# Mixture-of-experts block: the first layer's weighted rows stored in tile order and gathered per token

## The chip, the cores and the metric

The kernel runs on one core of one Trainium2 chip. The metric is the device time of one execution in microseconds; lower is better. The kernel before was timed three times: 865.56, 866.69 and 867.43 us, median 866.69 us.

## The reference

The input is `x`, 8 sequences of 512 tokens with 128 features. Three sublayers follow each other, each on a layer norm of `x`: half a feed-forward layer, causal attention with 16 heads, and the same half feed-forward layer again.

```
x = x + 0.5 * ffn(layernorm(x))
x = x + attention(layernorm(x))
x = x + 0.5 * ffn(layernorm(x))        # the same weights

ffn(x):  xn       = layernorm(x) * gamma + beta
         abel_out = gelu(xn @ abel_w + abel_b)
         topw, topi = top_k(xn @ moe_gate_w + moe_gate_b, 2); topw = softmax(topw)      # 8 experts
         expert e(t) = gelu(xn @ ew1[e] + eb1[e]) @ ew2[e] + eb2[e]                     # 128 -> 256 -> 128
         moe_out  = (sum over the token's two experts of topw * expert) @ expm(g0) @ expm(g1) @ expm(g2)
         gate     = sigmoid([abel_out, moe_out] @ gc_w + gc_b)
         return x + abel_out * (1 - gate) + moe_out * gate
```

## The kernel before, in words

**Units.** A chunk `c` is one sequence of 512 tokens (four tiles of 128). Both feed-forward layers route: each token is written twice, once per chosen expert, into the DRAM tensor `z_rows`, in the region of its expert. A row has 132 numbers: 128 features, the expert's weight, the row's own place (`Z_PLACE`, which says to which token and pick it belongs), and two spare ones. So an expert's rows lie together, and tiles of 128 rows with one expert each are read back. There are 80 tiles in a layer; four tiles are a quad (20 quads), two are a pair (`p`, 40 pairs). Rows of chunks 0 and 1 make run 0 in the first layer (quads 0 to 5), those of chunks 2 to 7 run 1 (quads 6 to 19).

**The expert stage** goes over the pairs. For each quad SyncE (SP) reads the tiles' starts from a table and issues four transfers of 66 KB into one of six x buffers (`load_x`, L654). TensorE transposes the quad (`x_turn`, L2080) at pair 2(q-1), ScalarE writes it (L1112), TensorE multiplies by `w1` of the tile's expert (`up`, L2106), ScalarE applies gelu (L1133), TensorE multiplies by the second matrix, which already holds the rotation (`down`, L2120 and L2122), and VectorE weights the rows into one of five y buffers (`y_out_`, L1630), two pairs behind in its own list. VectorE also copies the `w1` of each tile to a ring of five (L1677), three to four tiles ahead of its pair number. In its program order TensorE's pair `p` is `up(p)`, then the transposes if `p` is even, then `down(p-1)`, then what stands beside it.

**What becomes of y.** GpSimd (POOL) sends each tile of y with an indirect transfer to `y_rows`, which is ordered by token and pick; the index is the `Z_PLACE` column in the x buffer (`send_y`, L833). The x buffer of quad q-6 is free, and `load_x(q)` goes out, when these four have landed (`y_sent`). When a run is complete SP reads a chunk's pairs back with one plain transfer of 528 KB (`load_sums`, L618), after `load_x(0, 11)` for chunks 0 and 1, after the operands of batch 0 for chunk 2, and within the attention batches for the rest. `sum_pairs` adds the two picks of each token, and `finish_x` applies the gate and adds to `x`: on VectorE for chunks 0 and 1 (at p = 21 to 24 of its list), on GpSimd for chunks 2 to 7.

**Attention** goes over 8 batches of 40 units. The scores are computed twice, first for the row maxima (VectorE, L1757 to L1762), a batch ahead, then for the exponentials (ScalarE, L1194). For batch 0 SP writes the first half of the operands (`operands`, L541, L547, L551: 15 small transfers and one for zeros) as soon as VectorE has split q and k (`q_k_low(0)`, at p = 34), and TensorE starts the maxima's scores of batch 0 (L2204) when they have landed and its experts are done. In a batch GpSimd cuts the causal triangle out of the exponentials (`triangle`, L864; three instructions a call, eight calls a batch), and TensorE's products with v (`values`, L2276) wait for it. Between the triangles GpSimd sends the second layer's rows (`send_z`, L783): the first pick behind the last triangle of a batch, the second between the first two of the next.

**Other transfers.** During the first experts ScalarE's queue brings the attention's position biases, 1 MB each, at pairs 4, 6, 10, 12, 14, 16, 18, 20, 36 and 38 (`load_bias`, L1060, L1070). They and SP's transfers use queues q10 and q1 of the same 16 DMA engines; GpSimd's use q0.

The lists of all engines are written out by hand; `beside_experts` has, per engine, what stands at which pair.

## Time and profile before

| | us |
|---|---|
| median of three runs | 866.69 |
| the profiled execution's own time | 872.2 |
| its span | 870.4 |
| TensorE busy in the span | 684.1 (79%) |
| VectorE / ScalarE / GpSimd busy | 563.2 / 414.2 / 495.2 |
| indirect transfers of y, both layers (L833), GpSimd | 160 in 163.9 |

All durations below are from the one profiled execution. Its own time is 1.8 us above its span and 5.5 us above the median of the runs, so a sum is made against 872.2 us, and the same difference is then taken off the median. TensorE's granted clock over the span is 0.918 of full speed. The stages of the span: preparation to 118 us, the first experts from 135 to 264 us, the maxima of batch 0 from 268 to 295 us, the eight attention batches to about 690 us, then the second experts.

### The profile page before, as it was taken

The page shows a single profiled execution, that of the slowest core. Times are in us where ns is not written, and L with a number is a line of the kernel's source. Part 1 is how long each engine was busy: PE and PEld are TensorE (multiplying, and loading weights), DVE is VectorE, ACT ScalarE, POOL GpSimd, SP SyncE. Part 2 cuts the span into 40 slices and gives each one's busy share as a digit, 9 for nine tenths or more (in the row PEclk, how much of TensorE's full clock was granted, in tenths as well). Part 3 has the DMA queues.
Part 4 walks back from the last instruction along what each step waited for, and adds up shares of the span by engine and source line. Part 5 has one row for each costly group of instructions (what it writes and reads, how often), then busy time and mean ns, then how long its engine had stood idle before and what let it go on. Part 6 is the DMA issues. An engine that isn't in the chain of part 4 may idle for free.

```text
span 870.4 us, 18357 instructions
## 1 busy us (share of the span) xinstructions
PE 684.1 (79%) x5103; PEld 511.4 (59%) x5103; DVE 563.2 (65%) x2051; ACT 414.2 (48%) x931; POOL 495.2 (57%) x600
## 2 busy tenths in 40 slices
PE   1568637985898798999999999999986828888850
PEld 0468626875795564665656566565653418778850
DVE  3678852865857875776768677676772204687574
ACT  2246204543471264565655656555654715636530
POOL 2557773773685162456837477463545544567772
PEclk9969967997998998999999999999997969979985
DMA  8613342895257403114041230302100145333365
GB/s 243 198 42 91 101 108 75 230 254 183 71 135 188 128 21 93 24 27 128 2 120 35 51 103 16 95 9 69 49 14 29 34 115 140 98 89 93 105 213 165
DMA packets 84143, 86.59 MB, mean 99 GB/s; under 512 B 14561, under 2 KB 66412, under 8 KB 83692
## 3 DMA queue, kind: packets, MB, share of 16 engines
q1 hardware_dynamic: 64952, 50.14, 22.3%
q0 software_dynamic: 9312, 21.58, 7.3%
q10 hardware_dynamic: 9780, 13.69, 6.2%
q8 instruction: 45, 0.74, 0.4%
q14 instruction: 54, 0.44, 0.2%
HBM read 46.23 MB, written 31.92 MB: 90 GB/s over the span
## 4 chain that ended last, share of the span: by engine, by line
PE 48%; DVE 20%; issue 9%; DMA 7%; SPq 7%; ACT 4%; POOL 2%; ACTq 2%; DVEq 1%; POOLq 0%
PE bank L2276 8%; PE bank L2204 8%; PE bank L2251 7%; PE bank L2106 5%; DMA arena<-z_rows 3%; PE bank L2120 3%; PE pair L2047 3%; DVE mx L1757 2%; POOL y_rows L833 2%; SPq L551 2%; DVE mx L1759 2%; DMA y_rows<-arena 1%; PE bank L2080 1%; SPq L654 1%; DVE stat L1277 1%
## 5 line engine op out<-in xcount | busy, mean ns | idle before, releaser
L1194 ACT ACTIVATE arena<-bank 128x512 f32<-128x512 f32 x320 | 185.9, 600 | 168.9 <-PE bank L2251 166.1
L833 POOL DMA_INDIRECT y_rows<-arena x160 | 163.9, 1025 | 106.0 <-DVE arena L1630 70.7
L864 POOL TENSOR_SCALAR_AFFINE_SELECT arena<-arena 128x256 f32<-128x256 f32 (+1 forms) x192 | 94.6, 516 | 173.9 <-ACT arena L1194 173.8
L2204 PE MATMUL bank<-kZ,qT 128*128 128x512 f32 (+3 forms) x512 | 148.3, 357 | 14.1 <-DVE mx L1760 5.5
L2251 PE MATMUL bank<-qT,kZ 128*128 128x512 f32 (+3 forms) x512 | 155.9, 376 | 2.7 <-DMA qT<-mT_zero 2.0
L1133 ACT ACTIVATE arena<-bank,hidden_bias 128x128 f32<-128x128 f32 x320 | 91.3, 368 | 93.0 <-PE bank L2106 88.7
L2204 PEld LDWEIGHTS bank<-kZ,qT 128*128 128x128 f32 x512 | 87.5, 196 | 61.5 <-issue 17.9
L1757 DVE TENSOR_REDUCE mx<-bank 128x1 f32<-128x512 f32 x128 | 87.2, 681 | 41.4 <-PE bank L2178 40.4
L2106 PE MATMUL bank<-arena 128*128 128x128 f32 x640 | 95.1, 295 | 15.1 <-DVE arena L1677 8.9
L2120 PE MATMUL bank<-w_rot,arena 128*128 x640 | 100.9, 296 | 5.2 <-ACT arena L1133 5.2
L2276 PE MATMUL bank<-arena,vA 128*9 128x512 f32 (+3 forms) x1024 | 95.5, 453 | 11.8 <-issue 6.4
L2251 PEld LDWEIGHTS bank<-qT,kZ 128*128 128x128 f32 x512 | 84.8, 197 | 25.6 <-ACT arena L1194 11.1
L2106 PEld LDWEIGHTS bank<-arena 128*128 128x128 f32 x640 | 83.7, 204 | 22.7 <-issue 21.1
L783 POOL DMA_INDIRECT z_rows<-beside_kZ,place x80 | 78.7, 983 | 31.3 <-issue 22.0
L2120 PEld LDWEIGHTS bank<-w_rot,arena 128*128 128x128 f32 x640 | 89.7, 201 | 8.1 <-issue 6.4
L1677 DVE COPY arena<-w 128x256 f32 x160 | 46.6, 316 | 64.8 <-issue 35.8
L1759 DVE TENSOR_REDUCE mx<-bank 128x1 f32<-128x384 f32 x128 | 70.0, 547 | 16.4 <-PE bank L2181 16.1
L1630 DVE TENSOR_SCALAR arena<-bank,arena 128x132 f32<-128x132 f32 x160 | 48.8, 345 | 25.4 <-PE bank L2122 25.3
L2080 PE MATMUL bank<-ident,arena 128*128 128x128 f32 x160 | 28.2, 307 | 47.0 <-DMA arena<-z_rows 30.4
L1112 ACT ACTIVATE arena<-bank,cols 128x512 f32<-128x512 f32 x40 | 31.7, 792 | 64.4 <-PE bank L2080 64.4
L1762 DVE TENSOR_REDUCE mx<-bank 128x2 f32<-128x512 f32 x64 | 43.6, 681 | 18.2 <-PE bank L2184 13.3
L783 POOL DMA_INDIRECT z_rows<-w,place x48 | 46.8, 975 | 13.2 <-issue 11.3
(269 smaller groups left out, 1172.1 us busy)
## 6 DMA issues: line engine op xcount, KB each, us to landing
arena<-z_rows SPq DMA_DIRECT2D x160, 66.0 KB
kZ<-bias_k_r ACTq DMA_DIRECT2D x8, 1024.0 KB, 10.3
qT<-parts SPq DMA_DIRECT2D x42, 128.0 KB
kZ<-parts SPq DMA_DIRECT2D x168, 32.0 KB
sums<-y_rows SPq DMA_DIRECT2D x7, 528.0 KB, 5.2
beside_kZ<-y_rows SPq DMA_DIRECT2D x7, 528.0 KB, 7.6
y_rows<-arena POOLq DMA_INDIRECT x160
z_rows<-in_spare SPq DMA_DIRECT2D x4, 528.0 KB, 6.1
```

The lines of the kernel that those rows point to most:

```text
L783: g_.indirect_dma_start(z_rows[run], bass.IndirectOffsetOnAxis(place[g % DEEP][:, k, t:t + 1], 0), zz(g)[:, k, t, :], None).then_inc(z_sen ...
L833: g_.indirect_dma_start(y_rows[run], bass.IndirectOffsetOnAxis(x_[:, t, Z_PLACE:Z_PLACE + 1].bitcast(I32), 0), y_[:, t, :], None).then_inc ...
L864: g_.affine_select(out=cut, in_=cut, compare_op=ALU.is_ge, fill=0.0, base=0, pattern=[[0, 2], [0, blocks], [1, P]], channel_multiplier=-1) ...
L1133: a_(hid[p % 2][:, i, j, :], ps_up[p % 2][:, P * n:P * (n + 1)], ACT.Gelu, bias=hidden_bias[:, j, bass.ds(e, 1)]).then_inc(hidden_ok.sem, 1)
L1194: a_(dst, src, ACT.Exp).then_inc(exp_ok.sem, 1)
L1757: v.tensor_reduce(mx[:, 3, q, t:t + 1], src[:, :], AX.X, ALU.max).then_inc(reduced.sem, 1)
L1759: v.tensor_reduce(mx[:, 2, q, t:t + 1], src[:, 0:384], AX.X, ALU.max)
L2106: last = mm(into, tile(w1_e, j), tile(xnT[q % 2], t), start=True, stop=True)
L2120: mm(into, hid[p % 2][:, i, j, :], w2_rot[:, bass.ds(e, 1), j, :].rearrange("p a n -> p (a n)"), start=(j == 0), stop=False)
L2204: mm(outp, qT[u][:, t, query_tile * P:(query_tile + 1) * P], kZ[u][:, h, 0:keys], start=start, stop=False, skip_group_check=(kind != "full"))
L2251: return mm(outp, kZ[u][:, h, lo:lo + P], qT[u][:, t, lo:SEQ], start=start, stop=True, skip_group_check=(kind != "full"))
L2276: last = mm(ps_o[32 * q:32 * q + HD + 1, kb * P:SEQ], vA[u][:, kb, NG * q + t, :], pT[t % 2][:, q, PT_KB[kb]:PT_KB[kb] + n], start=(kb == ...
```

## The change

It concerns the first layer only; the second still scatters its y as before.

- `y_rows` of runs 0 and 1 are now in the order of the tiles. SP stores a whole quad with one plain transfer of 264 KB (`store_y`), once its four tiles are weighted, and signals `y_kept`. In SP's list `store_y(q-6)` stands ahead of `load_x(0, q)`, which no longer waits for anything sent. Quads 14 to 17 are stored ahead of the operands of batch 0, quads 18 and 19 behind them.
- The 80 indirect sends of the first layer go from GpSimd. In their place it gathers, per chunk, two picks of four tiles, each with an indirect transfer of 128 rows (66 KB), straight into the terms of the sum (`gather`): 64 for the eight chunks. Chunks 0 and 1 are gathered when quads 1 to 5 are stored, chunk 2 when quad 19 is and chunk 0 is finished, chunk 3 when chunk 2 is finished, chunks 4 to 7 in batches 0 to 3, two transfers behind each of the four last triangle calls.
- Where a row lies in tile order is worked out by VectorE: the place in the expert's region minus the expert's offset (`y_places`, three instructions per run, at p = 2 and p = 4). For this the picks and the places of the eight chunks are kept.
- `load_sums` of the first layer is gone; only the 256 KB of gelu terms of chunks 2 to 7 are still loaded (`load_abel_act`). Chunk 2 uses the buffers of chunks 3 to 7 rather than its own.
- On VectorE `sum_pairs(0, 0)` moves from p = 21 to 20, `sum_pairs(0, 1)` from 22 to 23, `finish_x(0, 0)` from 23 to 22, `finish_x(0, 1)` from 24 to 25, and the preparation of attention on all engines is two pairs earlier.
- ScalarE's first exponential waits for the last five stores where it waited for chunk 2.

```diff
--- before.py
+++ after.py
+    z_rows = dram_rows("z_rows", [(REGION + P) * E] * len(RUN_CHUNKS))
+    y_rows = dram_rows("y_rows", [NT * P * SWITCH[0], NT * P * (QUADS - SWITCH[0])] + [SPARE + 2 * E * P] * 2)
...
             n = QUADS * layer + q
-            engine.wait_ge(y_sent[n % Y_BUFS], 16 * NT * (n // Y_BUFS + 1))
+            if n < QUADS:
+                engine.wait_ge(y_kept[n % Y_BUFS], 16 * (n // Y_BUFS + 1))
+            else:
+                engine.wait_ge(y_sent[n % Y_BUFS], 16 * NT * len(range(n, QUADS - 1, -Y_BUFS)))
...
+            def load_abel_act(c):
+
+                if c == 2:
+                    wait(sp, y_weighted, 0)
+                else:
+                    x_done(sp, 0, c - 1)
+                sp.wait_ge(ab_stored, 16 * CH)
+                sp.dma_start(terms(0, c)[1], abel_act[SEQ * c:SEQ * (c + 1), :].rearrange("(t p) d -> p t d", p=P)
+                             ).then_inc(abel_act_in, 16)
+
...
+            def store_y(q):
+
+                run, n = run_of_quad(0, q)
+                up_to(sp, y_weighted, 0, NT * (q + 1))
+                sp.dma_start(y_rows[run][NT * P * n:NT * P * (n + 1), :].rearrange("(t p) n -> p t n", p=P),
+                             y_buffer(0, q)).then_inc(y_kept[q % Y_BUFS], 16)
...
-                if q >= X_BUFS:
+                if layer and q >= X_BUFS:
                     y_sent_up_to(sp, layer, q - X_BUFS)
...
             for q in range(X_BUFS, QUADS):
+                store_y(q - X_BUFS)
                 load_x(0, q)
-                if q == SWITCH[0] + X_BUFS - 1:
-                    load_sums(0, 0)
-                    load_sums(0, 1)
+            for q in range(QUADS - X_BUFS, QUADS - 2):
+                store_y(q)
             operands(sp, 0, 0, 0)
-            load_sums(0, 2)
+            for q in range(QUADS - 2, QUADS):
+                store_y(q)
+            load_abel_act(2)
...
-                    load_sums(0, b + 3)
+                    load_abel_act(b + 3)
...
+            def gather(c, picks=(0, 1), tiles=range(NT)):
+
+                run = run_of_chunk(0, c)
+                if 0 in picks and 0 in tiles:
+                    wait(pool, y_placed, run)
+                    last = SWITCH[0] if run == 0 else QUADS
+                    for q in range(last - Y_BUFS, last):
+                        y_sent_up_to(pool, 0, q)
+                    if c == 0:
+                        wait(pool, tabled, 1)
+                    if c >= 2:
+                        x_done(pool, 0, 0 if c == 2 else c - 1)
+                for k in picks:
+                    for t in tiles:
+                        g_.indirect_dma_start(terms(0, c)[0][:, t, k, :], None, y_rows[run],
+                                              bass.IndirectOffsetOnAxis(y_place[:, c, k, t:t + 1], 0)
+                                              ).then_inc(sums_in[1 if c == 1 else 0], 16)
...
-                if layer == 0:
-                    if p == 25:
-                        attention_roots(0)
-                        attention_roots(1)
-                    if p == 31:
-                        obias(0)
-                    if p == 34:
-                        obias(1)
-                    if p == 36:
-                        v_place(0, 0)
...
+            def first_experts():
+
+                for b in range(2):
+                    gather(b)
+                for b in range(2):
+                    attention_roots(b)
+                obias(0)
+                obias(1)
+                v_place(0, 0)
+                gather(2)
+                sum_pairs(0, 2)
+                finish_x(0, 2)
+                gather(3)
...
-                triangle(b, 2, 0)
-                triangle(b, 2, 2)
-                triangle(b, 3, 0)
-                triangle(b, 3, 2)
+                for i in range(4):
+                    triangle(b, 2 + i // 2, 2 * (i % 2))
+                    if b + 4 < BATCH:
+                        gather(b + 4, (i // 2,), range(2 * (i % 2), 2 * (i % 2) + 2))
...
-                    x_done(act, 0, 2)
-                    wait(act, y_weighted, 0)
+                    for quad in range(QUADS - Y_BUFS, QUADS):
+                        y_sent_up_to(act, 0, quad)
...
+            def y_places(r):
+
+                run, c = Run(dve, y_placed, r), slice(SPLIT[0] * r, SPLIT[0] if r == 0 else CH)
+                wait(dve, tabled, r)
+                n = RUN_CHUNKS[r] * 2 * NT
+                picks = pick_of[:, c, :, :, :].rearrange("p c k t e -> p (c k t) e")
+                run.step(v.tensor_tensor(picks, picks, offsets[r][:, 0:E].unsqueeze(1).to_broadcast([P, n, E]), ALU.mult))
+                run.join()
+                run.step(v.tensor_reduce(y_shift[:, c, :, :].rearrange("p c k t -> p (c k t)"), picks, AX.X, ALU.add))
+                run.join()
+                run.step(v.scalar_tensor_tensor(y_place[:, c, :, :], y_shift[:, c, :, :], -1.0, place_of[:, c, :, :], ALU.mult, ALU.add))
...
-                    if p == 21:
+                    if p == 2:
+                        y_places(0)
+                    if p == 4:
+                        y_places(1)
+                    if p == 20:
                         sum_pairs(0, 0)
                     if p == 22:
-                        sum_pairs(0, 1)
-                    if p == 23:
                         finish_x(0, 0)
                         attention_stats(0)
-                    if p == 24:
+                    if p == 23:
+                        sum_pairs(0, 1)
+                    if p == 25:
                         finish_x(0, 1)
                         attention_stats(1)
+                    if p == 26:
+                        attention_norm(0)
                     if p == 28:
-                        attention_norm(0)
+                        x_low(0)
                     if p == 30:
-                        x_low(0)
+                        attention_norm(1)
                     if p == 32:
-                        attention_norm(1)
+                        q_k_low(0)
                     if p == 34:
-                        q_k_low(0)
-                    if p == 36:
                         x_low(1)
...
-                    for b, at in ((0, 29), (1, 35)):
+                    for b, at in ((0, 27), (1, 33)):
```

SP's list around the first operands, before; `qT` and `kZ` are the operands, `oT` holds the split q and k, and the last x quad is ahead of the first row:

```order
L654 DMA arena<-z_rows 128x132
L541 DMA qT<-mT_zero 8x2x512
L547 DMA qT<-oT 32x2x512
L551 DMA kZ<-oT 8x2x512 x4
L547 DMA qT<-oT 32x2x512
L551 DMA kZ<-oT 8x2x512 x4
L547 DMA qT<-oT 32x2x512
L551 DMA kZ<-oT 8x2x512 x4
L618 DMA arena<-y_rows 128x4x264
L621 DMA arena<-abel_act 128x4x128
```

The same place on SP after; `y_rows<-arena` is a stored quad:

```order
L671 DMA arena<-z_rows 128x132
L639 DMA y_rows<-arena 128x4x132 x4
L553 DMA qT<-mT_zero 8x2x512
L559 DMA qT<-oT 32x2x512
L563 DMA kZ<-oT 8x2x512 x4
L559 DMA qT<-oT 32x2x512
L563 DMA kZ<-oT 8x2x512 x4
L559 DMA qT<-oT 32x2x512
L563 DMA kZ<-oT 8x2x512 x4
L639 DMA y_rows<-arena 128x4x132 x2
L622 DMA w<-abel_act 128x4x128
```

Four stores, of quads 14 to 17, now stand between the last x transfer and the first operand.

GpSimd's list from the last triangles of batch 1 to the second triangle of batch 2, before:

```order
L864 AFFINE_SELECT arena<-arena 128x2x128 x2
L864 AFFINE_SELECT arena<-arena 128x2x256
L864 AFFINE_SELECT arena<-arena 128x2x128
L783 DMA z_rows<-w,place 34816x132 x4
L864 AFFINE_SELECT arena<-arena 128x2x128
L864 AFFINE_SELECT arena<-arena 128x2x256
L864 AFFINE_SELECT arena<-arena 128x2x128
L783 DMA z_rows<-w,place 34816x132 x4
L864 AFFINE_SELECT arena<-arena 128x2x128
```

The same place after; `sums<-y_rows,y_place` is a gather:

```order
L905 AFFINE_SELECT arena<-arena 128x2x128
L905 AFFINE_SELECT arena<-arena 128x2x256
L905 AFFINE_SELECT arena<-arena 128x2x128
L819 DMA sums<-y_rows,y_place 128x132 x2
L802 DMA z_rows<-w,place 34816x132 x4
L905 AFFINE_SELECT arena<-arena 128x2x128
L905 AFFINE_SELECT arena<-arena 128x2x256
L905 AFFINE_SELECT arena<-arena 128x2x128
L802 DMA z_rows<-w,place 34816x132 x4
L905 AFFINE_SELECT arena<-arena 128x2x128
```

Two gathers now stand between the last triangle of the batch and the four sends of z.

## Rows read from the trace of the kernel before

**Rows 1.** Busy time by stretch; columns: PE, PEld, DVE, ACT, POOL, clock, DMA share, GB/s.
```profile
164.00:208.00 44.00, 29.42 (x238) 27.53 (x238) 28.78 (x113) 18.86 (x58) 28.17 (x27) 0.89 0.92 252
398.00:450.00 52.00, 49.38 (x375) 31.25 (x376) 38.72 (x121) 30.33 (x57) 33.33 (x46) 1.00 0.25 65
```

**Rows 2.** Waits, 134 to 270 us: total us, times, longest.
```profile
PE bank L2080 <- DMA arena<-z_rows: 14.1, 5, 9.5
```

**Rows 3.** Timeline of TensorE: start, us, line, [idle before it, releaser].
```profile
162.53 1.13 PE L2106 MATMUL bank<-arena 128*128 128x128 f32 x8 [0.23 <-ACT arena L1133]
172.35 1.13 PE L2106 MATMUL bank<-arena 128*128 128x128 f32 x8 [0.30 <-ACT arena L1133]
...
197.18 1.13 PE L2106 MATMUL bank<-arena 128*128 128x128 f32 x8
207.81 1.11 PE L2080 MATMUL bank<-ident,arena 128*128 128x128 f32 x4 [9.51 <-DMA arena<-z_rows]
...
215.96 1.13 PE L2106 MATMUL bank<-arena 128*128 128x128 f32 x8
...
222.40 2.05 PE L2106 MATMUL bank<-arena 128*128 128x128 f32 x8 [2.85 <-DVE arena L1677]
```

**Rows 4.** SP's own waits from 118 to 280 us, then its timeline.
```profile
SPq L650 <- DMA y_rows<-arena: 32.4, 9, 8.2
```
```profile
168.18 3.65 SPq L654 DMA_DIRECT2D arena<-z_rows  x4
179.25 9.57 SPq L654 DMA_DIRECT2D arena<-z_rows  x8
```

**Rows 5.** DMA queues, 164 to 208 us: packets, MB, share of the engines.
```profile
q10 hardware_dynamic: 3168, 6.29, 54.9%
q1 hardware_dynamic: 4966, 2.92, 26.2%
q0 software_dynamic: 850, 1.79, 10.9%
```

**Rows 6.** Chain that ended last: start, us, what was waited for.
```profile
171.16 10.38 DMA arena<-z_rows
...
186.72 2.21 DMA y_rows<-arena
```

**Rows 7.** Timeline of VectorE.
```profile
170.07 0.62 DVE L1630 TENSOR_SCALAR arena<-bank,arena 128x132 f32<-128x132 f32 x2
...
201.43 0.71 DVE L1605 TENSOR_TENSOR sums<-sums 128x528 f32<-128x528 f32 x1 [4.40 <-DMA sums<-y_rows]
...
254.21 0.62 DVE L1630 TENSOR_SCALAR arena<-bank,arena 128x132 f32<-128x132 f32 x2 [0.69 <-PE bank L2122]
```

**Rows 8.** Groups by line on GpSimd, 134 to 265 us, then its timeline.
```profile
L833 POOL DMA_INDIRECT y_rows<-arena x73 | 75.9, 1040 | 55.1 <-DVE arena L1630 40.5 <-issue 14.5
```
```profile
169.10 1.16 POOL L833 DMA_INDIRECT y_rows<-arena  x1 [0.30 <-issue]
```

**Rows 9.** Timelines of SP and of TensorE where attention starts.
```profile
250.12 0.93 SPq L541 DMA_DIRECT2D qT<-mT_zero  x1
...
258.92 3.14 SPq L551 DMA_DIRECT2D kZ<-oT  x4
```
```profile
264.40 0.22 PE L2122 MATMUL bank<-expert_bias,fixed 128*128 x1
268.16 0.80 PE L2204 MATMUL bank<-kZ,qT 128*128 128x512 f32 x1 [3.54 <-DMA kZ<-oT]
```

**Rows 10.** Timelines of GpSimd and TensorE at the start of batch 2.
```profile
400.02 1.09 POOL L783 DMA_INDIRECT z_rows<-w,place  x1 [0.19 <-issue]
...
405.87 1.40 POOL L864 TENSOR_SCALAR_AFFINE_SELECT arena<-arena 128x256 f32<-128x256 f32 x3 [0.96 <-ACT arena L1194]
...
412.22 1.40 POOL L864 TENSOR_SCALAR_AFFINE_SELECT arena<-arena 128x256 f32<-128x256 f32 x3
```
```profile
412.89 1.05 PE L2276 MATMUL bank<-arena,vA 128*9 128x512 f32 x8
```

More of the change, by code:

```diff
@@ L166, in macaron_block, with dram_rows @@
                   ident_c, bias_q_c, bias_k_c, fixed_c, spare_c, out):
-    z_rows, y_rows = ([nc.dram_tensor(f"{n}{run}", (rows_, ROW), FP32, kind="Internal").ap() for run in range(len(RUN_CHUNKS))]
-                      for n, rows_ in (("z_rows", (REGION + P) * E), ("y_rows", SPARE + 2 * E * P)))
+    def dram_rows(name, counts):
+        return [nc.dram_tensor(f"{name}{run}", (n, ROW), FP32, kind="Internal").ap() for run, n in enumerate(counts)]
+    z_rows = dram_rows("z_rows", [(REGION + P) * E] * len(RUN_CHUNKS))
+    y_rows = dram_rows("y_rows", [NT * P * SWITCH[0], NT * P * (QUADS - SWITCH[0])] + [SPARE + 2 * E * P] * 2)
     abel_in, abel_act = (nc.dram_tensor(n, (CH * SEQ, D), FP32, kind="Internal").ap() for n in ("abel_in", "abel_act"))
@@ L235, in macaron_block @@
         n_of = tiles_of = sb("n_of", [P, E])
-        first_tile, offset, jump = (sb(n, [P, E + 1]) for n in ("first_tile", "offset", "jump"))
+        first_tile, jump = (sb(n, [P, E + 1]) for n in ("first_tile", "jump"))
+        offsets = [sb(f"offset{i}", [P, E + 1]) for i in range(2)]
         tables = [sb(f"table{i}", [P, 2, MOST_TILES], I32) for i in range(2)]
@@ L441, in macaron_block @@
         abel_added = Steps(sem("abel_added"), 10 * CH)
-        sums_in = [sem(f"sums_in{i}") for i in range(3)]
+        y_placed = Steps(sem("y_placed"), 3)
+        abel_act_in = sem("abel_act_in")
+        y_kept = [sem(f"y_kept{i}") for i in range(Y_BUFS)]
+        sums_in = [sem(f"sums_in{i}") for i in range(2)]
         last_sums_in = [sem(f"last_sums_in{c}") for c in range(CH)]
@@ L526, in sums_in_up_to @@
             if layer == 0:
-                i, n = ((c, 32 if c == 2 else 16) if c < 3 else (0, 16 + 32 * (c - 2)))
+                one = 16 * 2 * NT
+                i, n = (c, one) if c < 2 else (0, one * c)
+                if c >= 2:
+                    engine.wait_ge(abel_act_in, 16 * (c - 1))
                 engine.wait_ge(sums_in[i], n)
@@ new lines, in load_abel_act, with load_sums @@
+            def load_abel_act(c):
[6 more added lines that the diff above has]
+                             ).then_inc(abel_act_in, 16)
+            def load_sums(c):
+                if c in (0, SPLIT[1]):
+                    last = SWITCH[1] if c == 0 else QUADS
+                    for q in range(last - Y_BUFS, last):
+                        y_sent_up_to(sp, 1, q)
+                pairs = y_rows[run_of_chunk(1, c)][2 * SEQ * c:2 * SEQ * (c + 1), :].rearrange(
+                    "(t p k) n -> p t (k n)", t=NT, p=P)
+                sp.dma_start(terms(1, c)[0].rearrange("p t k n -> p t (k n)"), pairs).then_inc(last_sums_in[c], 16)
@@ L825, in experts, with beside_experts @@
-            def experts(layer):
+            def beside_experts(p):
+                if p == 4:
+                    gate_roots(2 * CH - 1, 1)
+                    gate_roots(2 * CH - 1, 0)
+                if 14 <= p < 18:
+                    send_z(2 * CH - 1, ((p - 14) // 2,), range(2 * (p % 2), 2 * (p % 2) + 2))
+            def first_experts():
[10 more added lines that the diff above has]
+                gather(3)
@@ L915, in _ @@
             skip_roots_(1)
-            experts(0)
-            sum_pairs(0, 2)
-            finish_x(0, 2)
+            first_experts()
             over_batches(pool, batch)
-            experts(1)
+            experts()
         @block.scalar
@@ L1547, in gate_place @@
                     z_sent_up_to(dve, g - DEEP)
-                run.step(v.tensor_copy(place[g % DEEP][:, :, :], place_f[:, :, :]))
+                run.step(v.tensor_copy(place[g % DEEP][:, :, :], into))
                 run.end()
@@ L1566, in make_table @@
                 run = Run(dve, tabled, r)
-                layer, n, table = r // 2, 2 * NT * RUN_CHUNKS[r] + E, tables[r % 2]
+                layer, n, table, offset = r // 2, 2 * NT * RUN_CHUNKS[r] + E, tables[r % 2], offsets[r % 2]
                 wait(dve, counted, r)
@@ L2357, in beside_experts @@
                 if layer == 0:
-                    for b, at in ((0, 29), (1, 35)):
+                    for b, at in ((0, 27), (1, 33)):
                         if p == at:
```

64 lines of the change are left out of this document (22 added, 42 removed).

## The prediction, written before the changed kernel was timed

> **What bounds the kernel now.** I read the busy time by stretch first, then the waits of the stretch that stands out, then the timelines of the engines that meet there. In the attention batches TensorE is busy 49.38 of 52.00 us and the DMA engines a quarter of the time [rows 1]: there a wait of TensorE's is paid in full, and transfers are cheap. From 164 to 208 us, in the middle of the first experts, it is the reverse: TensorE is busy 29.42 of 44.00 us and the DMA engines 0.92 of the time [rows 1]. TensorE waits there for x quads, 14.1 us in five waits, the longest 9.5 us [rows 2].
>
> How much is lost there can be read from the starts of `up`. From pair 10 (162.53) to pair 14 (172.35) a pair takes 9.82/4 = 2.45 us. Pair 22 starts at 197.18, pair 25 at 215.96, pair 26 at 222.40 [rows 3]. At 2.45 us from pair 14 they would stand at 191.9, 199.3 and 201.7. So 16.7 us are lost by pair 25 and 20.7 us by pair 26; no change to this stage is worth more than 20.7 us.
>
> Two things make the loss. First, a quad of x is asked for late: SP waits 32.4 us in nine waits for scattered y [rows 4]. The send at 169.10 is the last of quad 4 [rows 8], and SP's next x transfer, which needed it, goes out at 179.25 [rows 4]. Second, what is asked for arrives slowly, since q10 with the biases has 54.9% of the engines, q1 26.2% and q0 10.9% [rows 5]: a quad whose last transfer had been issued at 171.16 lands 10.38 us later [rows 6], and quad 12, queued behind the two loads of sums, is waited for 9.51 us at 207.81 [rows 3].
>
> **The middle of the first experts.** Removed from POOL here are the sends, 73 in this stage at 1.040 us [rows 8] plus 0.30 us of issue each, 1.34 us. None of it is on TensorE's path by itself; what is on it is x waiting for them. Now x of quad q goes out right behind the weighting of quad q-6. Quad 5 is weighted at 170.7 (170.07 + 0.62) [rows 7], so x of quad 11 is asked for at about 173 and not behind 185. The two loads of sums, 1.06 MB, are no longer in front of quad 12.
>
> What comes late next is the gather. `sum_pairs(0, 0)` stands at VectorE's p = 20, which it reaches about when TensorE has done pair 19, 172.35 + 6 x 2.45 = 187 us; VectorE then stands until chunk 0 is there, and behind it in its list are the copies of w1 for pairs 22 and on, so TensorE stops at pair 22. The time is: quad 5 lands (L), eight gathers, the last one's landing, and 1.7 us for the sum (0.71 us for its first instruction [rows 7], about as much for the second long one, and a copy of w1). Then eight more gathers for chunk 1 and the same again for pair 25. No row shows a gather; the nearest is the scatter, 1.34 us each [rows 8], so eight take 10.7 us. A scatter's landing has 2.21 us [rows 6] as its lower end; the upper is 7.5 us, since 179.25 less about 1.5 us of SP's table reads is 7.5 us behind the end of the send at 169.10 + 1.16 [rows 4, 8]. I take 4 us for the first, 3 us for the second.
>
> L is the unknown that decides. The store of quad 5 can be issued at 171.3. If it were served at once it would land 2 to 3 us later, but ahead of it in q1 stand parts of x quad 9, y of quad 4 and x quad 10, and from 165 on the biases take their share. q1 carried 4966 packets in 44 us [rows 5], 113 a microsecond; a quad stored and a quad loaded are 512 rows each. About 1800 such packets from 166 us on are 16 us, so L = 182, and 2 us more for the slowest engine give 184. The bounds are 178 (q1 gets the share that q0 had too) and 190 (it gets a third less).
>
> With L = 184: chunk 0 issued at 195, landed at 199, pair 22 at about 201; chunk 1 issued at 205.7, landed at 208.7, pair 25 at 208.7 + 1.7 = 210.4, against 215.96. That is 5.5 us earlier. Pair 26 lost another 4 us before (6.44 us against 2.45), 2.85 of it waiting for VectorE [rows 3], which then had two finishes and two statistics in two pairs. They now stand at p = 22 and 25, and I count 2 us as won. In sum -7.5 us. With L = 178 it is 6 us more, -13.5; with 190 pair 25 comes at 216.4, and -1.5 is left.
>
> **Added on VectorE:** six small instructions of `y_places`, on 128 and 384 numbers, beside pairs 2 and 4, where its list has no other work. The nearest row is 0.71 us for 528 numbers [rows 7], so they are below 6 x 0.71 = 4.3 us, and I take 2 us in two places. VectorE is busy 28.78 of 44.00 us even in the fuller stretch that follows [rows 1], and is up to two pairs ahead with w1. I take 0; without that cover it would be 2 us.
>
> **The start of attention.** SP starts the operands of batch 0 at 250.12 and issues the last four from 258.92 to 262.06, 11.9 us in all; TensorE's experts end at 264.6 and it starts at 268.16, 3.54 us after waiting for them [rows 9]. Now `store_y(17)` stands ahead, which needs pair 35 weighted. Before, that is at 254.21 + 0.62 = 254.8 [rows 7], which is 9.8 us before the experts' end. Since the projections of batch 1 are now two pairs earlier, 1.5 us of them no longer lie between, so it is 8.3 us before the end. Then 0.6 us for the store and 11.9 us of operands: the last is issued 4.2 us after the experts' end, where it was 2.5 us before it. That is 6.7 us later. Before, the last landed 6.1 us behind its issue (268.16 - 262.06), with two biases of 1 MB under way; those keep their pairs and are through by then, so that the least landing of a transfer, 2.2 us as in [rows 6], is nearer. The start is then 6.4 us behind the experts' end and not 3.5: +3 us (bounds 2 and 6.7). Nothing hides it: VectorE and TensorE both have only the maxima to do, and the first exponentials wait for them.
>
> The gather of chunk 2 (issued once quad 19 has landed), its sum and finish, and the gather of chunk 3 are two times 10.7 us and some 10 us between, from about 7 us behind the experts' end. GpSimd is done by 38 us behind it. The first triangle comes behind the maxima (27 us, from 6.4 us behind the end on), their transfer and five exponentials, at about 40. I take 0; the cover is the maxima of batch 0, and without it all 10.7 us of chunk 3 would count.
>
> **The batches.** POOL gets eight gathers in each of batches 0 to 3, 10.7 us beside 18.7 us of idle time (52.00 - 33.33) [rows 1]. That hides them where the idle time lies behind them. At the end of the batch it does not: there two gathers, 2.6 us, stand ahead of four sends of z and the first triangle of the next batch. At batch 2 the sends began at 400.02, the triangle at 405.87 after 0.96 us of idle time, the second triangle at 412.22 with none, and TensorE's `values` at 412.89, right behind its first third (412.22 + 0.47) [rows 10]. So 2.6 - 1.0 = 1.6 us of delay reach that triangle, and 1.4 to 1.6 us TensorE. This holds for batches 2, 3 and 4 (batch 1 has no sends in front): 3 x 1.4 = +4.2 us. The bounds are 0 (a gather is issued faster than a scatter) and 6.
>
> **The sum:** -7.5 + 3 + 4.2 = -0.3 us on the profiled execution's 872.2, so 871.9; on the median of 866.69, 866.4. I say 866.
>
> A rule speaks on L. In rows, x alone in q1 was slow while q10 was full [rows 5, 6]. The Trainium skill, "DMA: Bandwidth & Descriptors", section "Queues, rings and completion order", says that each DMA engine takes turns between the queue rows that have work and serves a ring in order. By that rule y in q1 gives up q0's turn and stands ahead of x. It would move L and quad 11 towards the late bound, where the bytes alone (264 KB either way) would leave them alone. The trace agrees so far that x waited behind the sums.
>
> **Rivals.**
> 1. *Deeper loading pays in full* (22%). q1 had few rows outstanding from 171 to 179 us, since SP was waiting; with more asked for it gets more. For it: between 164 and 208 us it moved 2.92 MB, more than its x alone, while the sums were queued. L is then 178 and the middle wins 13.5; if the gathers also cost less in the batches, the costs are 5 us. 866.7 - 8.5 = 858 us, at most 864.
> 2. *y and x in one queue* (25%, the slower side). The two quads in q1 are 1024 packets in a pair of pairs of 4.9 us, 209 a microsecond, where 113 were carried; while biases are issued, x and the stores fall behind. Against it: when TensorE stands, no more biases are issued. It decides from L = 189 on: the middle gives 1.5 us or less, and the costs of 7.2 stay, +5.7 us: 872.4 us. With the operands at their upper bound 876.
> 3. *The scatter was hidden anyway* (5%): the DMA engines are at 0.92 and the bytes are the same, so pair 25 does not move, and the triangles have slack after all: 866.7 + 3 = 869.7 us.
>
> **Chances.** The forecast case (48%) runs from 862 to 870 us. A measurement of this kernel can tell 0.2% from no change, 1.7 us. Of the forecast's 48 points 19 lie below 865.0, 24 within, 5 above 868.4. With rival 1 wholly faster, rival 2 slower by 22 of 25 and 3 within, and rival 3 slower, faster has 0.41, same 0.27, slower 0.32. The range, 858 to 874, takes in rival 1's time and most of rival 2's; the forecast's own is 862 to 870.
>
> **What would show it.** In the profile after: TensorE's wait for `arena<-z_rows` falls below 8 us, and a wait of VectorE for `sums<-y_rows` of some 10 us stands in its place; pair 25 starts near 210 us; the gathers take 1.3 us each; TensorE starts batch 0's maxima 6 to 7 us behind the last expert product; and `values` waits for POOL 1.4 us in batches 2, 3 and 4. I am wrong if quad 5 lands before 178 or after 190 us, if the operands land with the experts' end, or if `values` shows no wait for POOL.

## The result, and the profile after

The changed kernel takes 872.06 us (median of 9 runs, 870.09 to 877.18), the kernel before 867.05 (9 runs beside it). The ratio is 1.0067, interval 1.0042 to 1.0093: slower, where 866 and no change were forecast. Measured a second time, on another chip, it was 870.47 against 866.16, ratio 1.0053 [1.0026, 1.0080]. The cost is 4 to 5 us. Executions more than 1.5% above the fastest of the same kernel (five later ones of 908 to 2911 us, and six of the kernel before in experiment 5) are left out of all medians and ratios.

By stage, each number the difference of two rows' starts in one execution, the last up to the span's end (the second column of before is the same kernel once more; its run took 866.29 us, near the median, where the one that the prediction rests on took 872.2):

| us | before | before again | after | after again |
|---|---|---|---|---|
| to the experts' first transposes | 134.95 | 134.04 | 133.14 | 134.03 |
| first experts | 129.45 | 125.18 | 120.73 | 122.04 |
| their end to the first maxima | 3.76 | 3.70 | 9.29 | 8.93 |
| to the first exponential | 31.90 | 32.26 | 33.12 | 33.00 |
| to the last `values` | 397.94 | 398.41 | 402.30 | 400.05 |
| to the span's end | 172.40 | 170.91 | 170.82 | 169.85 |
| span | 870.4 | 864.5 | 869.4 | 867.9 |

The mean of the experts falls by 5.9 us; the start of attention costs 5.4, the stretch to the first exponential 1.0, the batches 3.0. Preparation and the stretch behind the batches are 0.9 and 1.3 us shorter.

**The middle.** Busy time by stretch of after, columns as in [rows 1], then the same stretch in the second trace of before:

```profile
164.00:208.00 44.00, 34.54 (x282) 32.44 (x281) 32.41 (x139) 21.73 (x68) 16.99 (x17) 0.92 0.87 254
```
```profile
164.00:208.00 44.00, 34.59 (x279) 32.61 (x277) 30.46 (x126) 20.91 (x64) 28.27 (x28) 0.92 0.91 251
```

TensorE does 5.1 us more work there than in [rows 1], at nearly the same bytes per second, but the second trace of before has as much: this row does not show a gain. The table shows it, from the first transposes to the end of the experts. TensorE's waits of after, 134 to 270 us (total, times, longest), then VectorE's:

```profile
PE bank L2167 <- DVE arena L1734: 9.6, 5, 6.0
PE bank L2265 <- DMA kZ<-oT: 9.1, 1, 9.1
```
```profile
DVE sums L1662 <- DMA sums<-y_rows,y_place: 6.3, 1, 6.3
```

No wait for x is left, where [rows 2] had 14.1 us and the second trace of before 7.3. The wait has gone over to VectorE, which stands in front of `sum_pairs(0, 0)` with the copies of w1 behind it. The chain that ended last, of after (start, us, what):

```profile
168.74 8.47 DMA y_rows<-arena
...
178.16 1.06 POOL sums L819
...
187.30 6.49 DMA sums<-y_rows,y_place
193.81 0.72 DVE sums L1662
```

The store of quad 5 goes out right behind its weighting and lands 8.47 us later, at 177.21. Eight gathers are issued, the last from 187.30 to 188.34; the first read of their sums starts 5.5 us behind that. TensorE's `up` of pairs 22, 25 and 26 in after, against 197.18, 215.96 and 222.40 in [rows 3]:

```profile
195.67 2.05 PE L2167 MATMUL bank<-arena 128*128 128x128 f32 x8 [5.97 <-DVE arena L1734]
...
206.19 1.13 PE L2167 MATMUL bank<-arena 128*128 128x128 f32 x8 [0.55 <-ACT arena L1151]
...
210.26 1.13 PE L2167 MATMUL bank<-arena 128*128 128x128 f32 x8 [0.98 <-issue]
```

**The start of attention.** SP and TensorE of after, answering [rows 9]:

```profile
229.14 16.93 SPq L639 DMA_DIRECT2D y_rows<-arena  x4
246.19 0.94 SPq L553 DMA_DIRECT2D qT<-mT_zero  x1
...
255.36 2.81 SPq L563 DMA_DIRECT2D kZ<-oT  x4
258.21 1.40 SPq L639 DMA_DIRECT2D y_rows<-arena  x2
```
```profile
263.16 0.79 PE L2265 MATMUL bank<-kZ,qT 128*128 128x512 f32 x1 [9.06 <-DMA kZ<-oT]
```

SP holds the operands, whose inputs VectorE has written by 235.0, behind four stores until pair 35 is weighted. The last operand is issued by 258.2 and used at 263.16, 5.0 us later. The DMA engines are full there, with a busy share of 0.99 from 255 to 264 us. The queues of that stretch (packets, MB, share):

```profile
q1 hardware_dynamic: 1824, 1.28, 53.3%
q10 hardware_dynamic: 672, 1.13, 45.6%
```

In q1 two stores of 264 KB stand right behind the operands. Through q10 ScalarE sends its own half of the operands, issued from 251.92 on, behind a bias issued at 250.05.

**To the first exponential.** TensorE's first score of batch 0, before and after:

```profile
299.52 0.50 PE L2251 MATMUL bank<-qT,kZ 128*128 128x512 f32 x1 [1.99 <-DMA qT<-mT_zero]
```
```profile
295.45 0.79 PE L2312 MATMUL bank<-qT,kZ 128*128 128x512 f32 x1 [2.21 <-DMA qT<-mT_zero]
```

It waits for the transfer of the maxima. That took 3.01 and 2.97 us in the two traces of before and 3.86 and 3.79 us in the two of after. The score itself took 0.50 us at a granted clock of 1.00 before, and 0.79 and 0.80 us at 0.50, the lower of the two levels, after.

**The batches.** GpSimd and TensorE of after, where batch 1 ends and batch 2 starts, answering [rows 10]:

```profile
393.83 1.40 POOL L905 TENSOR_SCALAR_AFFINE_SELECT arena<-arena 128x256 f32<-128x256 f32 x3 [2.40 <-ACT arena L1233]
395.40 0.94 POOL L819 DMA_INDIRECT sums<-y_rows,y_place  x1 [0.17 <-issue]
396.65 0.94 POOL L819 DMA_INDIRECT sums<-y_rows,y_place  x1 [0.30 <-issue]
397.90 1.00 POOL L802 DMA_INDIRECT z_rows<-w,place  x1 [0.30 <-issue]
...
402.75 1.41 POOL L905 TENSOR_SCALAR_AFFINE_SELECT arena<-arena 128x256 f32<-128x256 f32 x3
...
409.14 1.42 POOL L905 TENSOR_SCALAR_AFFINE_SELECT arena<-arena 128x256 f32<-128x256 f32 x3
```
```profile
409.69 1.05 PE L2337 MATMUL bank<-arena,vA 128*9 128x512 f32 x8 [1.34 <-ACT arena L1233]
```

From the gathers to the second triangle GpSimd never idles, and `values` waits 1.34 us. The row names ScalarE as the releaser, but its wait ended 0.08 us after the triangle's first third (409.14 + 0.47). The same wait stands at 463.28 and 516.87 and nowhere later: three batches, as forecast. From batch 1 to 2, 2 to 3 and 3 to 4 this product comes 53.59 us after its predecessor; in the second trace of before a batch takes 51.8 to 52.1. The three together are 5.0 us longer.

### The profile page after: what moved, and what is told of

The parts are those of the page before. It is cut to its first block, busy times and chain, and to the rows that moved or that the text cites. A ratio compares the mean times of both kernels' runs of the same rounds, so it can differ in the third digit from the quotient of the medians.

```text
span 869.4 us, 18390 instructions
## 1 busy us (share of the span) xinstructions
PE 678.1 (78%) x5103; PEld 506.2 (58%) x5103; DVE 566.7 (65%) x2057; ACT 414.1 (48%) x931; POOL 474.5 (55%) x584
## 4 chain that ended last, share of the span: by engine, by line
PE 47%; DVE 22%; issue 10%; DMA 5%; SPq 5%; ACT 4%; POOL 3%; ACTq 2%; DVEq 1%; POOLq 0%
PE bank L2337 8%; PE bank L2265 8%; PE bank L2312 7%; PE bank L2167 5%; PE bank L2181 3%; PE pair L2108 3%; DVE mx L1814 2%; DVE mx L1816 2%; SPq L563 2%; DMA y_rows<-arena 2%; POOL y_rows L874 2%; DVE arena L1687 1%; DVE stat L1316 1%; PE pair L2360 1%; ACT arena L1233 1%
## 5 line engine op out<-in xcount | busy, mean ns | idle before, releaser
L819 POOL DMA_INDIRECT sums<-y_rows,y_place x56 | 54.5, 972 | 99.1 <-DMA y_rows<-arena 84.2
L874 POOL DMA_INDIRECT y_rows<-arena x80 | 80.1, 1002 | 47.7 <-DVE arena L1687 28.8
L2181 PE MATMUL bank<-w_rot,arena 128*128 x640 | 98.7, 291 | 6.9 <-ACT arena L1172 6.5
L2181 PEld LDWEIGHTS bank<-w_rot,arena 128*128 128x128 f32 x640 | 87.7, 197 | 10.3 <-issue 8.9
L1151 ACT ACTIVATE arena<-bank,cols 128x512 f32<-128x512 f32 x40 | 31.8, 795 | 51.8 <-PE bank L2141 51.8
L802 POOL DMA_INDIRECT z_rows<-w,place x48 | 46.9, 977 | 13.5 <-issue 12.0
```

The source lines that it names most:

```text
L802: g_.indirect_dma_start(z_rows[run], bass.IndirectOffsetOnAxis(place[g % DEEP][:, k, t:t + 1], 0), zz(g)[:, k, t, :], None).then_inc(z_sen ...
L874: g_.indirect_dma_start(y_rows[run], bass.IndirectOffsetOnAxis(x_[:, t, Z_PLACE:Z_PLACE + 1].bitcast(I32), 0), y_[:, t, :], None).then_inc ...
L2181: mm(into, hid[p % 2][:, i, j, :], w2_rot[:, bass.ds(e, 1), j, :].rearrange("p a n -> p (a n)"), start=(j == 0), stop=False)
```

## The experiments

Ratios are to runs of before on the same chip, and are not exactly the quotients of the medians. Experiments 1 to 4 share one chip, experiment 5 has another and experiment 6 a third.

**1. The kernel before, once more.**

> The kernel before, unchanged, for a second trace. Theory A: the profiled execution shown ahead of the prediction (872.2 us, 5.5 above the median) was a slow one of its kind, and its surplus lies in places that the change does not touch: preparation (134.95 us to the first x transposes) and tail (30.9 us from the last expert product to the end); a second trace shows about 133 and 28 us there, and an own time of 866 to 869. Theory B (rival): a profiled execution is always some 5 us longer than a plain one; then it is again near 872. Ratio to the kernel before 1.000 in both.

No edit. 867.19 us, ratio 1.0007 [0.9976, 1.0038]. Its waits, 134 to 270 us:

```profile
PE bank L2080 <- DMA arena<-z_rows: 7.3, 3, 5.3
PE bank L2106 <- DVE arena L1677: 7.2, 6, 2.3
```

The wait for x is half that of [rows 2], and the experts are 4.3 us shorter. The profiled execution took 866.29 us, so theory B is out. Theory A had the time right and the place wrong: of the 5.9 us between the two spans 0.9 lie in preparation and 2.4 behind the last expert product of the second layer (28.6 us against 31.0), but 4.3, the largest part, in the very stage that the change relieves. In the second trace the other stretches are 1.6 us longer in sum. The size of 4.3 us rests on this one pair of traces, and whether both ran on one chip is not known.

**2. Operands first**, a change of the order of SP's list alone:

```diff
-            for q in range(QUADS - X_BUFS, QUADS - 2):
-                store_y(q)
+            store_y(QUADS - X_BUFS)
             operands(sp, 0, 0, 0)
-            for q in range(QUADS - 2, QUADS):
+            for q in range(QUADS - X_BUFS + 1, QUADS):
                 store_y(q)
```

> The changed kernel with the operands of batch 0 issued behind store_y(14) and ahead of store_y(15) to (19). Theory A: the 9.1 us that TensorE waits for kZ<-oT after its last expert product come from the stores of quads 15 to 17, which wait for pair 35, standing ahead of the operands; SP can then start them when q and k are split, some 11 us earlier, they land before the experts end, and the wait falls below 1 us: 8 to 9 us faster than the changed kernel, 863 to 864 us. Theory B (rival): the transfers are slow to land because of the two late biases and of the stores in the same queue, and issuing them earlier gains only part, 2 to 4 us: about 869 us.

865.00 us, ratio 0.9990 [0.9970, 1.0011], 5.5 to 7 us less than the changed kernel (870.47 and 872.06), between the two theories and nearer to A. TensorE in this kernel at the start of attention:

```profile
256.34 0.47 PE L2264 MATMUL bank<-kZ,qT 128*128 128x512 f32 x1 [1.28 <-DVE arena L1686]
```

SP starts the operands at 236.07, 10 us earlier. The 9.06 us wait for them is gone; 1.28 us for VectorE's last weighting are left, and 0.9 us for a later operand.

**3. No gathers at the batch's end:**

```diff
-                        gather(b + 4, (i // 2,), range(2 * (i % 2), 2 * (i % 2) + 2))
+                        for j in ((0, 1), (2, 3, 4), (5, 6, 7), ())[i]:
+                            gather(b + 4, (j // 4,), (j % 4,))
```

> The changed kernel with the eight gathers of a batch behind the fifth, sixth and seventh triangle call (2, 3 and 3 of them) and none behind the eighth. Theory A: batches 2, 3 and 4 are 53.6 us and not 51.8 because two gathers delay the sends of z and with them the second triangle of the next batch; with none there the three batches return to 51.8 and 5 us are won: about 867 us. Theory B (rival): the batches are longer because POOL has 10 us more of work, or the DMA engines 0.5 MB more, wherever it stands; then they stay above 53 us and the time at 872.

867.35 us, ratio 1.0024 [0.9995, 1.0053], 3 to 5 us less than the changed kernel, at theory A's time. GpSimd at the same place:

```profile
396.74 1.40 POOL L905 TENSOR_SCALAR_AFFINE_SELECT arena<-arena 128x256 f32<-128x256 f32 x3 [1.93 <-ACT arena L1234]
398.31 1.00 POOL L802 DMA_INDIRECT z_rows<-w,place  x1 [0.18 <-issue]
...
404.20 1.40 POOL L905 TENSOR_SCALAR_AFFINE_SELECT arena<-arena 128x256 f32<-128x256 f32 x3 [1.03 <-ACT arena L1234]
```

The idle time in front of the triangle is back (1.03 us, [rows 10] had 0.96), and no `values` waits at these places. Three gathers in a row behind an earlier triangle cost little: two of the three batches take 52.2 us, against 53.6 in the changed kernel and 51.9 before. The other takes 53.0; in it the granted clock is 0.50, the lower level, from 394 to 396 us, behind a wait of 1.24 us that the changed kernel has too, at a clock of 1.00.

**4. Both edits.**

> The changed kernel with both edits: operands ahead of store_y(15), and no gather behind the last triangle. Theory A: the two costs are independent and add up, 9 + 5 us, so 858 to 860 us, 0.8 to 1.0% faster than the kernel before; what is left is the gain in the middle of the first experts. Theory B (rival): what is won before the batches is lost again, since the maxima of batch 0 then wait for something else (the second half of the operands, or GpSimd's chain of chunks 2 and 3, which starts later than the operands); then it is 863 us or more.

859.87 us, ratio 0.9931 [0.9909, 0.9952]; measured again in the last set, 860.42, ratio 0.9939 [0.9916, 0.9962]. This beats both kernels. The two costs are separate waits and add up: 12.2 us below 872.06, where the single edits took off 7.1 and 4.7. Theory A.

**5. The first set on the middle.** These four kernels ran on another chip, on which before takes 967.15 us (959.07 to 973.12, 23 runs); there is no profile of before from there, so only their ratios and their own waits are read. Ratio and quotient of the medians differ by up to 0.4% here. In the first, x of the first layer waits for its store again:

```diff
-                if layer and q >= X_BUFS:
+                if q >= X_BUFS:
                     y_sent_up_to(sp, layer, q - X_BUFS)
```

> The changed kernel, but SP asks for x of quad q (first layer) only once the store of quad q-6 has landed, as the kernel before did with its sends. Theory A (the gain in the middle is the earlier asking for x, and the rest that TensorE still loses there is VectorE's wait for the gathered sums): a store lands about 4 to 7 us behind its issue, so quads 11 to 13 are asked for later by that, a wait of TensorE's for x of 4 to 10 us comes back between 180 and 210 us, quad 5 is not stored earlier, and the last expert product stands 2 to 6 us later relative to the first transposes of the experts than after's 120.7 us. Rival B (the gain comes from the two loads of sums, 1.06 MB, that no longer stand in front of quad 12; when x is asked for is worth nothing): no wait for x above 1.5 us, the last expert product at 120.7 +- 1 us. By A 874 to 878 us, by B 871 to 873 us, against 872 for the changed kernel.

983.94 us, ratio 1.0213 [1.0169, 1.0257], above the 874 to 878 us of theory A (1.008 to 1.013 of before). Two waits for x came back, 6.2 us in sum.

The second is before, with `load_sums(0, 0)` and `load_sums(0, 1)` behind x of quad 12 (`q == SWITCH[0] + X_BUFS` in place of `- 1`):

> The kernel before, with the loads of the sums of chunks 0 and 1 behind x of quad 12 in SP's list and not ahead of it. Theory A (the loads of sums delay quad 12, and this is one part of the loss in the middle): TensorE's longest wait for x, 9.5 and 5.3 us in the two traces of before, shrinks to below 4 us, but VectorE then waits longer for the sums than its 4.4 us, 6 us or more, so that pairs 22 and on stand: the time is within 2 us of before, 865 to 869 us. Rival B (the loads are what costs the middle): the last expert product comes 5 us or more earlier relative to the first transposes than 125.2 to 129.5 us, 860 to 863 us.

971.01 us, ratio 1.0068 [1.0031, 1.0105]. Only 0.3 us of waiting for x are left in its trace; VectorE waits 5.8 us for the sums. So the loads moved out of x's way do not pay here, and rival B is out. The ratio lies above what theory A allowed (the medians give 1.0040), and on this chip I can't say where the rest went.

The third is experiment 4 with the sums later on VectorE (the gate's tanh on ScalarE goes along, to pairs 22 and 25):

```diff
-                    if p == 20:
+                    if p == 22:
                         sum_pairs(0, 0)
-                    if p == 22:
+                    if p == 24:
                         finish_x(0, 0)
                         attention_stats(0)
-                    if p == 23:
+                    if p == 25:
                         sum_pairs(0, 1)
-                    if p == 25:
-                        finish_x(0, 1)
-                        attention_stats(1)
                     if p == 26:
                         attention_norm(0)
+                    if p == 27:
+                        finish_x(0, 1)
+                        attention_stats(1)
```

> The changed kernel with the operands first and no gathers at the batch's end (859.9 us), and with the two sums of chunks 0 and 1 and their finishes one to two pairs later in VectorE's list (sums at p = 22 and 25, finishes at 24 and 27). Theory A (what TensorE still loses at pair 22 is VectorE standing 6.3 to 7.3 us in front of sum_pairs(0, 0), with the copies of w1 behind it): two pairs are 4.9 us, so VectorE's wait falls from 7.3 to about 2.4 us, TensorE's stop at pair 22 goes, and the last expert product stands 3 to 5 us earlier relative to the first transposes than 121.9 us; 855 to 857 us. Rival B (the x quads or the second chunk's gather are what comes late next, so the loss only moves to pairs 25 to 27): VectorE's wait for the sums moves, TensorE's waits in sum stay at 10 us or more, the time within 1.5 us of 859.9.

963.25 us, ratio 0.9961 [0.9925, 0.9997].

The fourth has p = 21, 23, 24 and 26 there:

> As sums_late, but one pair later each (sums at p = 21 and 24, first finish at 23, second at 26 together with the norm of chunk 0). Theory A: VectorE's wait falls by 2.45 us to about 4.9 us, and TensorE's stop at pair 22 by as much: 857 to 858 us, between both_moved and sums_late. If both steps give as much as the wait that they take away, the wait was all that stood at pair 22. Rival B: no difference to both_moved, 859.9 +- 1 us, and none to sums_late either.

964.83 us, ratio 0.9997 [0.9967, 1.0027]. The two intervals overlap, and experiment 4 had not run on that chip: inconclusive. I repeated what mattered.

**6. The second set**, on a chip where before takes 866.16 us (23 runs).

> The changed kernel, unchanged, as the partner of the next three on the same chip. On a chip where before takes 867 us: 872 us, ratio to before 1.007, DVE's wait for the gathered sums 6 us in the middle, the last expert product 120 to 121 us behind the first transposes. On one that takes 968 us for before, where all engines stop for about 20 us together in the first experts, the same steps should cost the same microseconds: ratio 1.003 to 1.008.

870.47 us, ratio 1.0053 [1.0026, 1.0080], as told above. VectorE waits 7.4 us for the gathered sums.

> The changed kernel with the operands first and no gathers at the batch's end, measured again beside the others. Theory A: 12 us less than after_again (872.1 - 859.9), ratio to before 0.993 again, since both terms are waits with a fixed place. Rival B: part of those 12 us was chance between executions, the ratio is 0.997 or more.

860.42 us, 10.1 less than the changed kernel beside it, where theory A had 12 and a ratio of 0.993. The ratio of 0.9939 is theory A's.

> The changed kernel with x of quad q asked for only once the store of quad q-6 has landed, once more beside the changed kernel itself (the first measurement, 1.021 of before, had no run of the changed kernel on its chip). Theory A (asking early is what the middle gained): 6 to 14 us more than after_again, with a wait of TensorE's for x of 4 us or more between 180 and 215 us. Rival B (the loads of sums gone from in front of quad 12 are what it gained): within 2 us of after_again.

887.50 us, ratio 1.0257 [1.0220, 1.0293]: 17.0 us more than the changed kernel, above theory A's own 14. Rival B is out. The experts take 137.55 us (133.28 to 270.83). TensorE, then SP in total, of this kernel:

```profile
175.53 1.12 PE L2141 MATMUL bank<-ident,arena 128*128 128x128 f32 x4 [3.70 <-DMA arena<-z_rows]
...
184.24 0.66 PE L2141 MATMUL bank<-ident,arena 128*128 128x128 f32 x4 [1.74 <-DMA arena<-z_rows]
...
193.11 0.66 PE L2141 MATMUL bank<-ident,arena 128*128 128x128 f32 x4 [4.05 <-DMA arena<-z_rows]
...
202.14 0.66 PE L2141 MATMUL bank<-ident,arena 128*128 128x128 f32 x4 [2.70 <-DMA arena<-z_rows]
```
```profile
SPq L667 <- DMA y_rows<-arena: 48.1, 13, 7.6
```

The quads come 8.9 us apart, (202.14 - 175.53)/3, where TensorE wants one each 4.9: store, landing, load, landing stand in a row in SP's list. The row also holds up the stores: the gathers start at 194.90 and VectorE waits 9.7 us for the sums, so the 17 us are not the wait for x alone. With plain stores it is the asking ahead, for x and with it for the next store, that carries the middle; the store alone, waited for, makes it much worse than the scatter did.

> both_again with the two sums and their finishes one to two pairs later in VectorE's list, beside both_again on the same chip. Theory A (what is left in the middle is VectorE waiting for the gathered sums with the copies of w1 behind it): VectorE's wait of 7.3 us falls to 2.4 us or less, 2 to 5 us less time than both_again. Rival B (the time comes back at pairs 25 to 27): TensorE's waits for VectorE's w1 stay at 10 us in sum, and the time within 1.5 us of both_again.

856.88 us (5 runs), ratio 0.9900 [0.9865, 0.9936], 3.5 less than `both_again` beside it, and the fastest kernel of this study. VectorE in this kernel:

```profile
195.06 0.71 DVE L1662 TENSOR_TENSOR sums<-sums 128x528 f32<-128x528 f32 x1 [2.22 <-DMA sums<-y_rows,y_place]
```

In `both_again` this row is at 197.88 with 9.88 us of waiting. TensorE's waits for w1 fell from 13.2 us to 2.7, the experts from 124.38 us to 118.86 (121.86 in the trace of experiment 4). Part of that is that the gathers start at 182.18 in `both_again` and at 177.87 here. Theory A, though the intervals of the two ratios still overlap a little.

## Why the prediction was wrong

**Right.** The transfer of the wait from x to the gathered sums; the sends' removal; one gather 0.95 + 0.30 = 1.25 us (1.34 taken from the scatter), up to 1.07 + 0.30 in the first experts; `y_places` at nothing (pair 10 starts 27.4 us behind the first transposes, 27.6 and 27.5 before); the late operands; the three batches.

**The middle, -7.5: the mechanism right, its parts off in both directions, the size about right against the trace it was read from.** L was taken as 184, from q1 keeping its 113 packets a microsecond. Quad 5 landed at 177.21, even before the bound of 178 that was rival 1's, which by the prediction's own list is a sign that it is wrong. It was stored at 168.74, 2.6 us earlier than reckoned. The queues of after, 164 to 208 us, answering [rows 5]:

```profile
q10 hardware_dynamic: 3134, 6.22, 45.4%
q1 hardware_dynamic: 7727, 3.79, 32.2%
q0 software_dynamic: 512, 1.08, 8.4%
```

With more asked of it, q1 got more, 176 packets a microsecond. In seven traces with this order of stores the gathers start between 177.87 and 182.18, so L is no constant. On the other side, the first use of the gathers came 5.5 us behind the end of the last issue, not 4. `up` of pair 25 stood at 206.19 (210.4 forecast). The end of the experts, from their first transposes, came 7.4 to 8.7 us earlier than in the trace that I had, but 3.1 to 4.5 us earlier than in the second trace of before.

The Trainium skill, "DMA: Bandwidth & Descriptors", section "Queues, rings and completion order", has the engines take turns between queue rows and serve a ring in order, and the prediction read it as speaking for a late L. L came early, and the stores in q1 did not hold x up: no wait for x. That q1 got more because more was outstanding is a reading and not shown; q0 also had fewer packets (512 against 850). No run here tells the two apart, nor turns between rows from shares by bytes.

**The step that failed first: taking the 5.5 us between the profiled execution and the median off the sum evenly.** The working ended on 871.9 against that execution's 872.2; the changed kernel's own profiled run took 871.24, near its median. So the sum was met on the profiled execution, and its last line, 871.9 to 866.4, was not: of those 5.5 us the larger part lay in the first experts (4.3 us between the two traces of experiment 1), in the wait that the change removes. The second trace, near the median, has half the wait for x, so the same change wins only half there: with the mean of both traces of after, 125.18 - 121.39 = 3.8 us instead of 7.5. That alone is 3.7 of the 5.7 us between 866.4 and 872.06. With one pair of traces the size is an estimate; that the step from 871.9 to 866.4 failed is shown by the medians.

**The operands, +3: mis-sized.** The place and the issue were right (last issue 4.1 us behind the experts' end, 4.2 forecast). The landing was taken as the least landing in the trace, 2.2 us, since no bias would be in the way; it was 5.0, so the wait grew by 5.4 (9.06 against 3.54, and 8.71 against 3.48 in the second pair), within the bounds of 2 to 6.7. The engines were full even so (0.99), with two stores, ScalarE's operands and what was left of the last bias; which of them delayed the landing no run tells. Experiment 2 shows that most of it and of the old wait too could go, for 5.5 to 7 us.

**The batches, +4.2: right.** 1.34 us of wait three times, 1.7 of period, 5.0 over the three; net of other differences 3.0 by the stage table, and 3.1 to 5.1 us by the runs (870.47 and 872.06 less 867.35; 865.00 less 859.87).

**Taken as nothing:** 1.0 us more from the first maxima to the first exponential, in both traces of after (33.1 and 33.0 against 31.9 and 32.3). Of it 0.8 us are the maxima's transfer and 0.3 the first score at the lower clock, less 0.1 of small differences. GpSimd's gathers of chunk 3, which the prediction put at nothing, are under way beside that transfer, but they are no sure cause: in experiment 3 they are too, and it took 3.22 us, and 3.00 in `x_waits_again`. The cause stays open.

Together, the mean of after against the second trace of before: -3.8 + 5.4 + 0.8 + 2.8 = +5.2, less 1.0 in preparation and behind the batches, +4.2, against +5.0 and +4.3 measured. Of the rivals none was it: x and y in one queue (rival 2) gives the size, 872.4, by a mechanism that didn't happen.

## What to carry to other kernels

When the profiled execution is slower than the median, look where: a wait on contended DMA varies from one execution to the next (here 14.1 against 7.3 us), and it must not be counted both as what the change wins and as what separates the profile from the median. A second trace of the same kernel is worth more than a finer sum on the first.

In a list written by hand, put a transfer whose input is ready ahead of one that waits, and an instruction that can stand anywhere where idle time lies behind it: a few lines of order were worth 10 to 12 us and turned a loss into a gain. When a wait moves to another engine, move its consumer too, up to where the next wait begins.

## What the runs showed of the hardware that I had not expected

On the chip of experiment 5 a kernel takes some 100 us more. Part of it is time in which TensorE, VectorE and ScalarE nearly stop together, with nothing that the profile shows as the cause, while GpSimd goes on issuing a gather each 1.25 us. One pair's `up` there, of the kernel with the sums at p = 21 (start, us, idle before), and the same 16 us by engine:

```profile
230.64 0.37 PE L2166 MATMUL bank<-arena 128*128 128x128 f32 x1 [1.78 <-issue]
233.45 0.37 PE L2166 MATMUL bank<-arena 128*128 128x128 f32 x1 [2.45 <-issue]
234.91 0.37 PE L2166 MATMUL bank<-arena 128*128 128x128 f32 x1 [1.08 <-issue]
237.05 0.37 PE L2166 MATMUL bank<-arena 128*128 128x128 f32 x1 [1.77 <-issue]
```
```profile
226.00:242.00 16.00, 4.16 (x18) 3.29 (x18) 1.19 (x5) 1.08 (x5) 9.47 (x10) 0.58 0.45 122
```

Eight matmuls that take 1.13 us elsewhere take 13 us. The granted clock over the profiled spans is 0.87 to 0.89 on that chip, 0.92 to 0.93 on the others. The cause is open; the lesson is to compare within one chip only.

A plain store of 264 KB landed 8.47 us behind its issue, and the first use of eight gathers came 5.5 us behind the end of the last issue, while q10 carried 6.22 MB in 44 us. The ten stores of 150 to 215 us took 2.7 to 13.5 us to land, median 7.2, where the 2.2 us of [rows 6] had been the least landing before.
